# One function table for exponential and logarithm, step sizes in one bundle, three banks for the first sequence

## The reference

```
# gating of layer 0
scores = sqrt(softplus(xt @ gate_w.T));  top 2 of scores + gate_b, weights from scores
# scan of layer 1, 512 channels, 16 states each
delta = softplus(dtl @ W_dt.T + b_dt + b_dt)        # the "step sizes"
x = silu(conv(x));  du = delta * x
for t: state = exp(delta_t * A) * state + du_t * B_t;  y_t = sum_n(state * C_t)
y = (y + x * D) * silu(z);  out = y @ W_out.T
```

## Time and profile before

| | us |
|---|---|
| median of 3 runs | 1937.45 (1933.76 to 1938.24) |
| the profiled execution's own time | 1933.68 |
| its span | 1931.9 |
| TensorE busy | 1602.0 (83%) |
| VectorE busy | 1545.5 (80%) |
| ScalarE busy | 1208.3 (63%) |
| GpSimd busy | 1001.8 (52%) |

### The profile page before, as it was taken

How to read it: one execution, slowest core, us unless ns; L and a number is a source line. 1 busy time by engine, 2 the same in 40 slices (tenths; PEclk the granted TensorE clock), 3 DMA queues, 4 the chain that set the end, 5 groups by cost and what they waited for, 6 DMA issues and landing times. The chain is left out here.

```text
span 1931.9 us, 22676 instructions
## 1 busy us (share of the span) xinstructions
PE 1602.0 (83%) x5880; PEld 713.8 (37%) x5948; DVE 1545.5 (80%) x2808; ACT 1208.3 (63%) x2037; POOL 1001.8 (52%) x796
## 2 busy tenths in 40 slices
PE   2266688848998899878998899889997999889857
PEld 0113223323552346233542345233632363235325
DVE  6664799858998889978998889888997869986840
ACT  3447757767667694858577685769576538644322
POOL 0010764473368635773469535873568327964630
PEclk9768799869999899989999999899999999989988
DMA  5000232311233212321232222321233214332300
GB/s 161 1 6 26 84 114 68 107 33 63 72 103 113 80 63 72 130 95 66 67 115 104 82 66 88 117 90 60 66 116 111 72 41 127 119 124 95 111 31 12
DMA packets 94729, 157.95 MB, mean 82 GB/s; under 512 B 11068, under 2 KB 23788, under 8 KB 94596
## 3 DMA queue, kind: packets, MB, share of 16 engines
q1 hardware_dynamic: 94596, 156.43, 24.6%
HBM read 143.83 MB, written 12.58 MB: 81 GB/s over the span
## 5 line engine op out<-in xcount | busy, mean ns | idle before, releaser
L1453 POOL TENSOR_TENSOR prod<-state,c_all 128x512 f32<-128x512 f32 x512 | 650.8, 1278 | 537.4 <-DVE state L1430 447.5
L1430 DVE TENSOR_TENSOR_SCAN state<-decay,ps_b 128x512 f32<-128x512 f32 x512 | 622.4, 1216 | 32.3 <-POOL prod L1453 4.0
L973 PE MATMUL ps_y<-prod,idf 128*128 128x512 f32 x1024 | 591.5, 669 | 24.6 <-POOL prod L1453 18.8
L1171 ACT ACTIVATE decay<-delta,a_neg 128x512 f32<-128x512 f32 x512 | 364.2, 721 | 251.8 <-DVE state L1430 248.0
L1437 DVE TENSOR_TENSOR ps_b<-du,ps_b 128x512 f32<-128x512 f32 x512 | 348.3, 680 | 75.2 <-PE ps_b L966 70.9
L966 PE MATMUL ps_b<-b_rows,sel_b 48*128 48x512 bf16 x512 | 203.2, 402 | 77.2 <-DVE state L1430 75.6
L973 PEld LDWEIGHTS ps_y<-prod,idf 128*128 128x128 f32 x1024 | 169.3, 199 | 169.0 <-issue 107.2
L966 PEld LDWEIGHTS ps_b<-b_rows,sel_b 48*128 48x128 bf16 x512 | 46.5, 93 | 376.7 <-DVE state L1430 275.8
L830 PE MATMUL ps_x<-xT,w 128*128 128x512 bf16 (+1 forms) x386 | 128.8, 412 | 36.1 <-DVE arena_l L1336 13.6
L944 PE MATMUL ps_x<-arena_b,fcT 128*128 128x512 f32 x256 | 127.3, 612 | 1.1 <-ACT arena_b L1150 0.7
L950 PE MATMUL ps_x<-pjT,arena_b 128*128 128x256 f32 x512 | 119.9, 384 | 4.2 <-ACT arena_b L1159 2.8
(11 more groups left out here) (238 smaller groups left out, 2362.3 us busy)
## 6 DMA issues: line engine op xcount, KB each, us to landing
c_all<-c_rows SPq DMA_DIRECT2D x512, 256.0 KB
c_rows<-arena_l SPq DMA_DIRECT2D x32, 256.0 KB
out<-arena_b SPq DMA_DIRECT2D x16, 256.0 KB
x_in<-in_base SPq DMA_DIRECT2D x8, 256.0 KB
c_all<-in_winT SPq DMA_DIRECT2D x1, 1280.0 KB, 7.3
arena_b<-in_w_fc SPq DMA_DIRECT2D x1, 1024.0 KB, 6.9
arena_l<-in_w_proj SPq DMA_DIRECT2D x1, 1024.0 KB, 9.0
w<-in_w1T SPq DMA_DIRECT2D x1, 792.0 KB, 9.6
```

Of the source, the lines that this page charges most:

```text
L973: nc.tensor.matmul(ps_y[:], idf[:], prod[:, n % NP, :], start=(n % NST == 0), stop=(n % NST == NST - 1)).then_inc(reduced, 1)
L1171: nc.scalar.activation(decay[:, n % NDA, :], delta[:, slot(s, ct), :], ACT.Exp, scale=a_neg[:, ct, st:st + 1]).then_inc(decayed, 1)
L1430: nc.vector.tensor_tensor_scan(state[:, n % NS, :], decay[:, n % NDA, :], ps_b[:, n % NDB, :], 0.0, ALU.mult, ALU.add).then_inc(scanned, 1)
L1453: nc.gpsimd.tensor_tensor(prod[:, n % NP, :], state[:, n % NS, :], c_all[:, n % NC, :], ALU.mult).then_inc(multiplied, 1)
```

## The change

The change removes the halves of steps, the order 0, 3, 1, 2 of the step sizes, and the account of table loads in the planner. It begins the four tiles of step sizes at the rounds 14, 15, 17 and 18, so that they overlap ("the bundle"). It asks for the set `natural_log_exp_and_others` before the first `d_exp` of a bundle and before `gate_exp`. It gives the attention of sequence 0 three banks in turn. The planner's costs are other numbers, and it has weights of its own for the last two iterations (`BUT_ONE`, `LAST`).

```diff
-D_ORDER = (0, CT - 1) + tuple(range(1, CT - 1))
-D_AT = tuple(D_ORDER.index(i) for i in range(CT))
...
+    d0 = (14, 15, 17, 18)
     for i in range(CT):
-        k = 15 + 9 * D_AT[i]
+        k = d0[i]
         steps += [(k, "P", ("d", i)), (k + 1, "A", ("d_abs", i)), (k + 2, "A", ("d_exp", i)), (k + 3, "A", ("d_one", i)),
                   (k + 4, "A", ("d_less", i)), (k + 5, "A", ("d_log", i)), (k + 5, "G", ("d_fix", i)), (k + 6, "G", ("d_sum", i)),
                   (k + 7, "G", ("delta", i)), (k + 8, "G", ("du", i))]
...
-FIRST_HALF = {"proj": "proj_a", "gram": "gram_a", "fc": "fc_a", "wout": "wout_a", "x4": "x4_a", "apply": "apply_a", "add": "add_a",
-              "gate_root": "gate_root_a"}
...
-EARLY, LATE, BACK, QUANT, GATE = (halved(r) for r in (early_rounds(), late_rounds(), back_rounds(), quant_rounds(), gate_rounds()))
+EARLY, LATE, BACK, QUANT, GATE = early_rounds(), late_rounds(), back_rounds(), quant_rounds(), gate_rounds()
...
-TABLE_LOAD = 128
-LOG_TABLE = ("log",)
...
-                if op in USES and USES[op] not in table:
-                    when, table = when + TABLE_LOAD, ("exp", "tanh")
...
-URGENT = {"late": (1.07, 0.00728, 16.8, 1.59, 10.8, 0.0792, 0.106, 0.0435),
...
+URGENT = {"late": (0.32, 0.21, 0.17, 1.42, 0.34, 0.61, 0.01, 0.02),
...
+def early_bank(s, step):
+
+    return (XE, 1, 2)[TURN_USES.index(step) % 3] if is_seq(s, 0) and step in TURN_USES else XE
...
-            if step in EARLY_BANK:
+            bank = early_bank(s, step)
+            if is_seq(s, 0) and step in TURN_USES:
+                k = TURN_USES.index(step)
+                if k >= 3:
+                    eng.wait_ge(early["A"], ea(s, "A", EARLY_BANK[TURN_USES[k - 2]]))
+                if name in READS:
+                    eng.wait_ge(early["A"], ea(s, "A", READS[name](i)))
+            elif step in EARLY_BANK:
                 eng.wait_ge(early["A"], ea(s, "A", EARLY_BANK[step]))
...
             elif name == "gate_exp":
+                nc.scalar.preload_act_table_set("natural_log_exp_and_others")
                 eng.wait_ge(early["A"], ea(s, "A", "gate_abs"))
...
             elif name == "d_exp":
+                if i == 0:
+                    nc.scalar.preload_act_table_set("natural_log_exp_and_others")
                 eng.wait_ge(late["A"], la(s, "A", ("d_abs", i)))
...
-            urgent = FIRST if held else URGENT
+            urgent = FIRST if held else (URGENT, BUT_ONE, LAST)[max(0, 2 - left)]
```

More of the change, by code:

```diff
@@ L268 @@
 BUSY = {
-    "A": {"b_turned": 91, "back apply_a": 98, "back apply": 98, "c_out": 48, "cw_turned": 48, "d_abs": 114, "d_exp": 54, "d_less": 61,
-          "d_log": 54, "d_one": 52, "dt_out": 48, "eps16": 19, "exp": 122, "f_turned": 48, "gate_abs": 17,
-          "gate_exp": 12, "gate_log": 14, "h_turned": 91, "late apply_a": 94, "late apply": 94, "p_out": 38, "probs": 122, "pv_out": 48,
-          "qk_out": 48, "raw": 48, "relu": 49, "round": 20, "shift": 123, "square": 53, "tanh": 49, "turned": 91,
-          "v_out": 48, "v_relu": 96, "w_out": 48, "wo_out": 48, "wo_relu": 96, "x4_a": 112, "x4": 112, "x_one": 52, "x_tanh": 57,
-          "x_turned": 91, "y_turned": 91, "z_tanh": 49},
@@ L287 @@
-SCAN_BUSY = {"decay": 62, "spread": 33, "drive": 60, "scan": 114, "product": 123, "pair": 122, "sum": 96, "taken": 66, "load": 6}
-TABLE_LOAD = 128
-LOG_TABLE = ("log",)
-USES = {"d_log": "log", "gate_log": "log", "d_exp": "exp", "gate_exp": "exp", "exp": "exp", "decay": "exp",
-        "tanh": "tanh", "x_tanh": "tanh", "z_tanh": "tanh"}
+    "A": {"apply": 196, "probs": 110, "v_relu": 110, "wo_relu": 110, "round": 30, "d_one": 52, "d_less": 52, "f_turned": 48, "p_out": 37, "relu": 48, "square": 52, "w_out": 48, "z_tanh": 49, "cw_turned": 48,
+          "exp": 122, "gate_abs": 15, "gate_exp": 12, "gate_log": 142, "pv_out": 47, "qk_out": 47, "raw": 47, "turned": 90,
+          "v_out": 47, "wo_out": 47, "x_turned": 106, "y_turned": 89, "b_turned": 89, "c_out": 48, "d_abs": 114,
+          "d_exp": 180, "d_log": 182, "dt_out": 48, "h_turned": 89, "tanh": 49, "x4": 224, "x_one": 52, "x_tanh": 58},
@@ L294 @@
+SCAN_BUSY = {"decay": 62, "spread": 33, "drive": 60, "scan": 114, "product": 125, "sum": 87, "taken": 66, "load": 6}
 HANDOVER = 12
@@ L453, in weave @@
         else:
-            uses = USES.get(name_of(st[3])) if e == "A" else None
-            if uses is not None and uses not in table:
-                when, table = when + TABLE_LOAD, LOG_TABLE if uses == "log" else ("exp", "tanh")
             when += busy(e, st[0], st[3])
```

221 lines of the change are left out of this document (104 added, 117 removed).

## The result

The changed kernel took 1922.65 us (median of 4 runs, 1921.29 to 1925.19), the kernel before 1937.72 beside it: a ratio of 0.9926, 95% interval 0.9911 to 0.9941. It is faster by 0.7%, where 1951 was forecast. The range (1917 to 1985) held it, the direction was wrong. Its profiled execution took 1921.29 us with a span of 1919.5, against 1933.68 and 1931.9: 12.4 us less of span.

The account below looks back on a forecast made before the run. Matmuls bind a steady iteration up to state 48, then the loop of scan and product. Terms −22 + 12 − 3 + 25 + 1 + 2.5 = +15.5 us gave 1949 profiled or 1953 median; forecast 1951, range 1917 to 1985.

Parts of the forecast that it names:

- The first state: Start of the first scan: gating root and step sizes now precede it, +12 us (bounds +5, +18); three banks −3.
- The last quarter: Steady iteration from state 48 on: more GpSimd and ScalarE work there, +6 us each, bounds +2.7 and +12.
- The tail: Back chain of the last sequence: whole adds wait for second halves, +2.5 us, bounds +1 and +4.
- The loads: Table loads on ScalarE: 84 instead of 79, 1.283 us each, 6.4 us more, costed within the last quarters.
- Iteration 6: Second-to-last iteration: last quarter +12 us, the three before −11, sum +1, bounds −6 and +8.
- Iteration 0: First iteration: its stateless 34.3 us hole closes, 197 us instead of 218.7, −22, bounds −10 and −33.
- A steady iteration, up to state 48: First three quarters of iterations 1 to 5: z.2 and z.3 leave TensorE, −1 us each, bounds −3.3 and +5.
- iteration 7: Last iteration: keeps its order nearly, 0 us, bounds −3 and +3.
- B: Rival: the hole closes and a shorter stretch up to state 48 hides the last quarter's load; 1924 us, chance 0.24.

## Why the prediction was wrong, by its own steps

**Right.** The first state: +8.1 of +9, at 218.9 as in the window named. The step sizes stand behind the root on GpSimd, as worked out from the earlier trace rows; the root itself is 5.43 us from 204.22 now. The last quarter: +7.7 an iteration, of +6 with bounds 2.7 and 12; GpSimd is busy 43.24 us against 43.9 reckoned, though 87% of the quarter and not the 90 that were named, and the runs with 39 loads less and with z twice show that neither ScalarE nor TensorE sets it. The tail: +2.1 of +2.5. The loads: 84, each 1.283 us, and hidden.

**Right by luck.** Iteration 6: 0 of +1, but as a sum of −18.1 up to state 48 and +18.1 after, where −11 and +12 were forecast. Both terms were 6 to 7 us too small, and they cancel. One sum of the prediction is wrong in itself: five times the upper bounds +5 and +12 are +85, not +75.

**Right in kind, off in size.** Iteration 0: −15.2 of −22. VectorE's work is 180.1 us where 181 was reckoned, but in a share of 88.5% of the time, not 92. The scan waits 12.9 us in the states of iteration 0, against 6.2 before:

```profile
L1414 DVE TENSOR_TENSOR_SCAN state<-decay,ps_b 128x512 f32<-128x512 f32 x64 | 77.8, 1215 | 12.9 <-ACT decay L1155 6.3 <-POOL prod L1437 3.7
```

Half of it is for decays, which now have the bundle among them on ScalarE. In the changed kernel, undoing the bundle brings the hole back and 11.6 us with it.

**The step that failed** is "A steady iteration, up to state 48: I take −1; bounds −3.3 and +5". It came out at −7.8 an iteration, 39.1 us over five, outside the bounds, and it paid the whole price of the last quarters (+38.7). The step counted what leaves the stretch on TensorE (z.2, z.3: 3.1 us), held the share of busy time, and wrote the moves inside the stretch off as "no change in sum". The count was right; what it held fixed was not. Up to state 48 the iterations 1 and 3 of the kernel before, then 1 and 3 of the changed one:

```profile
429.50:602.60 173.10, 163.81 (x670) 80.35 (x679) 156.24 (x299) 121.95 (x218) 87.20 (x69) 0.97 0.24 79
860.90:1028.00 167.10, 157.32 (x664) 75.90 (x672) 155.03 (x300) 120.87 (x216) 87.29 (x69) 1.00 0.25 82
```

```profile
422.40:582.90 160.50, 153.75 (x656) 74.30 (x655) 147.22 (x285) 112.55 (x203) 81.34 (x61) 1.00 0.27 91
848.20:1014.50 166.30, 160.25 (x661) 78.54 (x661) 147.96 (x284) 112.78 (x203) 81.23 (x61) 0.96 0.25 83
```

- *The count.* At a granted clock of 1.00 TensorE is busy 157.3 us before and 153.8 after: 3.6 less, z and little else. Over five iterations z is 15.5 of the 39.1 us.
- *The idle time.* TensorE's idle time falls from 47.4 us over the five to 31.7, by 15.7. Moving z alone raised it (see below), so the fall comes from the rest of the new order. The step had it at nothing.
- *The clock.* Within one order the stretch grows by what the clock takes: 167.1 us at 1.00 and 173.1 at 0.97 before, 160.5 at 1.00 and 166.3 at 0.96 after. The clock has two levels, 2.4 and 1.2 GHz, and the granted share is their mean; length times the missing share is an estimate of what it costs. With 0.981 on average over the five iterations before and 0.990 after it is 16 us and 8, so some 8 of the 39.1 go with the clock. The prediction has no term for it. For this row of the table, where the changed kernel has 811.3 us, three other traces with the same steady order (one bank, the weights of the last two, 45 loads) have 808.8 to 812.5, and the two without the requests 816.6 and 819.2. Of the kernel before there is one trace.

This is an account of where the time went, and four runs bear on what made it. The kernel before with just these z moved gets 0.5 us an iteration shorter there, since idle time grew by 6.5 us over four where busy time fell by 8.4: the count by itself is not the gain. TensorE's idle time in iteration 4 up to state 48 is 9.7 us before and 6.3 with the change; with the bundle but the weights of before it is 10.4 (in the kernel before) or 17.4 (in the changed one), and with the new weights but serial step sizes 11.7. So the bundle and the new weights give it only together. But each set of weights goes with its own plan and costs, so these runs don't say which of them does it.

What is different in the stretch can be read. The chain of the next sequence is shorter in rounds by 24 of 50, so h_turn can stand behind state 36 instead of 27, and the work before it spreads: the three parts of iteration 4 were 67.2, 60.8 and 42.5 us and are 55.0, 49.2 and 56.3. TensorE was busy for 92, 99 and 91% of them and is for 91, 100 and 97%; VectorE was busy for 88, 96 and 88% and is for 97, 88 and 90%. So before, both were fullest in the same part, and now in different ones. That this is why the idle time fell is an argument, not a result. VectorE is busy 39.0 us less over the five. Some 16 to 20 of these are not work that left but the same instructions made shorter: what they take beyond the lower quartile of their line and shape falls from 8.9 to 4.9 us an iteration. One kind in iteration 4 up to state 48, before and after, with the mean in ns behind the busy time:

```profile
L1206 DVE TENSOR_SCALAR arena_e<-arena_e,ri_a 128x256 bf16<-128x256 bf16 x4 | 1.9, 536 | 0.0
```

```profile
L1190 DVE TENSOR_SCALAR arena_e<-arena_e,ri_a 128x256 bf16<-128x256 bf16 x4 | 0.9, 280 | 0.0
```

Shorter instructions alone don't do it: the bundle alone has still fewer lengthened ones (4.0 us) and a longer stretch. Which steps of the new order matter stays open.

**The second miss** is iteration 7, "keeps its order nearly: 0". It doesn't: three proj and three gram, which stood together between the states 31 and 36, are spread over the states by weights of their own, worth 5.1 of the 7.0 us by the run without them.

**The rivals.** B was what happened (−12.4 in the profiled executions, against −4.5): its condition, "up to state 48 the iteration gets shorter by as much", is the measured one. That its time, 1924, is within 2 us of the measured one is luck: it had iteration 0 at −22 and iteration 7 at 0, which were −15.2 and −7.0. Its ground was GpSimd's waits for the scan, and no run shows that they were the room; what the rows show is TensorE's idle time. I gave it 0.24 because I priced that stretch by a difference of counts, with bounds that came from the same count.

## What to carry to other kernels

When a planner's weights change, a stretch in which one engine is over 90% busy must not be priced by the difference of what enters and leaves it alone: the same work of an iteration took 210.1 us in one order and 234.5 in another. Give such a stretch three terms: the count, the idle time of the fullest engine, and what its clock lost there. The rows before had all three for an iteration up to state 48 (3.1, 9.5 and 3.2 us, means over five). A lower bound of −3.3 took the first and left out the rest, so by it an order could use next to nothing of the other 12.7 us; the measured gain used 4.7 of them. And the rounds of one chain and the weights must be judged together.

Where an engine is the fullest in a stretch (GpSimd in the last quarter), counts gave the price of work put on it within 2 us. Moving work off it gave less than the count: 2.1 us for 5.1, and a loss once the next engine was as full.
